# A decoder layer on one core: last products added by VectorE, low halves read later, a first variance by squares, gate products behind Silu alone

## The reference

```python
# 1. attention-like mixing
Xn = layernorm(X) * gamma + beta
Q, K, V = split(Xn @ W_in + b_in, 3)
K, V = rotary(K), rotary(V)                       # the first 256 features turned
A = sum over tokens of (K / |K|) * (V / |V|)      # one number per batch and feature
Y = (0.5 * A + 0.5) * Q @ W_out + b_out + X       # x1 = layernorm(x + Y)
# 2. cross product with a context, both quantised to fp8 by their largest value
out = quantised(x1) @ quantised(ctx) + mask       # x2 = layernorm(x1 + out)
# 3. feed-forward with experts
mlp = silu(x2 @ gate_w) * (x2 @ up_w) @ down_w
routing: product keys, the 8 best of 64 x 64 pairs per token, index into 1024 rows
experts = sum over 8 rows of silu(x2 . down_row) * softmax(score) * up_row
result = layernorm(x2 + mlp + experts)
```

## Time and profile before

| | us |
|---|---|
| median of 3 runs | 812.98 (812.97 to 815.38) |
| profiled execution, its own time | 813.83 |
| span of the profiled execution | 812.0 |
| TensorE busy | 786.8 (97%) |
| VectorE busy | 675.4 (83%) |
| GpSimd busy | 372.2 (46%) |
| ScalarE busy | 314.4 (39%) |

### The profile page before, as it was taken

The page is one execution under the profiler, slowest core; times in us unless marked ns, Lnnn a source line. Parts: engine busy times, 40 slices in busy tenths (PEclk is TensorE's granted clock), DMA queues, the critical chain, the costliest instruction groups (busy, mean ns, idle before and its releaser), DMA issues. The chain is left out here.

```text
span 812.0 us, 10715 instructions
## 1 busy us (share of the span) xinstructions
PE 786.8 (97%) x3631; PEld 644.5 (79%) x3631; DVE 675.4 (83%) x1331; ACT 314.4 (39%) x688; POOL 372.2 (46%) x303
## 2 busy tenths in 40 slices
PE   8999999998899999999999999999999999999995
PEld 6878888887777778888888888888878877878784
DVE  6887679895799782277679999999999999999997
ACT  6444347353564413212343333333333333333322
POOL 1332122232233221113468667776666667677432
PEclk9999999997999999999999999999999999999998
DMA  8567505544446329100023231322333334222113
GB/s 321 223 144 168 104 17 126 144 105 78 54 129 147 63 96 315 44 1 31 30 78 90 83 91 39 120 71 67 99 94 89 92 92 115 70 79 71 37 55 153
DMA packets 51336, 81.70 MB, mean 101 GB/s; under 512 B 17520, under 2 KB 26480, under 8 KB 50769
## 3 DMA queue, kind: packets, MB, share of 16 engines
q0 software_dynamic: 24384, 33.48, 19.6%
q1 hardware_dynamic: 25312, 47.52, 16.9%
q10 hardware_dynamic: 1584, 0.01, 0.1%
HBM read 110.44 MB, written 12.58 MB: 151 GB/s over the span
## 5 line engine op out<-in xcount | busy, mean ns | idle before, releaser
L1718 PE MATMUL gu<-x_hi,w_hi 128*128 128x512 f32 x528 | 206.9, 392 | 2.2 <-DVE mid L1488 1.8
L1720 PE MATMUL gu<-x_hi,w_lo 128*128 128x512 f32 x528 | 205.5, 389 | 0.0
L1719 PE MATMUL gu<-x_lo,w_hi 128*128 128x512 f32 x528 | 205.5, 389 | 0.0
L1237 POOL TENSOR_TENSOR h_lo<-mid,h_hi 128x512 fp32r<-128x512 f32 x62 | 80.2, 1315 | 106.9 <-ACT h_hi L1357 106.4
L1367 ACT ACTIVATE gates<-dots 128x1 f32<-128x1 f32 x144 | 29.3, 203 | 232.2 <-DVE dots L1579 229.3
L1718 PEld LDWEIGHTS gu<-x_hi,w_hi 128*128 128x128 f32 x528 | 99.1, 188 | 25.2 <-DVE mid L1488 4.4
L1720 PEld LDWEIGHTS gu<-x_hi,w_lo 128*128 128x128 f32 x528 | 99.1, 188 | 20.9
L1719 PEld LDWEIGHTS gu<-x_lo,w_hi 128*128 128x128 f32 x528 | 99.2, 188 | 20.1
L1256 POOL DMA_INDIRECT ctx_q<-table_dram,row_i x64 | 80.4, 1256 | 62.2 <-DVE xall L1588 42.5
L1256 POOL DMA_INDIRECT scratch<-table_dram,row_i x64 | 82.8, 1293 | 39.5 <-issue 21.4
L1718 PE MATMUL ob<-w_hi,h_hi 128*128 128x512 f32 x248 | 97.4, 393 | 2.4 <-POOL h_lo L1237 2.4
(11 more groups left out here) (214 smaller groups left out, 1404.4 us busy)
## 6 DMA issues: line engine op xcount, KB each, us to landing
stage<-in_ctx SPq DMA_DIRECT2D x7, 1024.0 KB, 6.2
total<-prod POOLq DMA_DIRECT2D x12, 512.0 KB, 4.7
xall<-half_bo POOLq DMA_DIRECT2D x4, 1024.0 KB, 10.1
xhat<-in_L_ffn_gate_w SPq DMA_DIRECT2D x8, 512.0 KB
xhat<-in_L_ffn_up_w SPq DMA_DIRECT2D x8, 512.0 KB
xall<-in_mask_Bx1xS_ff POOLq DMA_DIRECT2D x4, 1024.0 KB, 10.8
xhat<-in_L_ffn_down_w SPq DMA_DIRECT2D x8, 512.0 KB
x_dram<-xall SPq DMA_DIRECT2D x4, 1024.0 KB, 8.4
```

Source lines behind the costliest of these rows:

```text
L1237: nc.gpsimd.tensor_tensor(lo[:, c], mid[c][:], hi[:, c].bitcast(F32), ALU.subtract).then_inc(hlo_done, 1)
L1718: nc.tensor.matmul(dst, lhs[0], rhs[0], start=start, stop=False)
L1719: nc.tensor.matmul(dst, lhs[0], rhs[1], start=False, stop=False)
L1720: return nc.tensor.matmul(dst, lhs[1], rhs[0], start=False, stop=stop)
```

## The change

- The last tile's products of the last batch no longer go through GpSimd's DMA: VectorE adds `prod` to `total` (`last_total`) when the second DMA has landed, and signals `total_all`, for which `token_sums(LAST)` waits. On VectorE the residuals 2 and 3 and their variance come ahead of this, `ctx_quantise(3)` behind it, and `low_ffn` behind `low_y`. On ScalarE `copy_sums(LAST)` comes behind two centres and scales.
- Products with a low part come later: in `key_value` (batch 0, and tile 0 of the others), in tile 0 of `attention`, in the first gate product of units 0 to 2, and in tile 0 of `down` and `down_early`. TensorE waits for the high part first, and for the low part ahead of its own products.
- The first batch's variance in the second block: the residual also sums its output, a one-column operation makes minus the mean (`minus_first`), ScalarE squares the centred tile and sums it (`deviation`), VectorE makes the variance (`first_variance`). Its transposes go to `ob`, those of the other batches stay in `gu`. Transposes of batch 1 and the cross products of batch 0 alternate. ScalarE's `scaled(1, (2, 3))` comes behind `high_x2(0)`.
- The low parts of the first down and query weights move from GpSimd to VectorE (`first_low_w`); GpSimd's next `low_w` waits for them.
- From unit 5 on the gate products wait for `silu_done` of the unit before, and the up products for `mid_done`.
- `keep_running`: 10 for 6 at the end of the first block; 5, 3 times 7, 4 and 3 for 8, 3 times 10, 4, 8 and 4 at the start of the second.

The core of the diff (16 columns of indentation are taken off; "..." marks what is left out):

```diff
-    add_products(b, 3)
+        add_products(b, 3)
...
 query(LAST, 0)
 query(LAST, 1)
-copy_sums(LAST)
 for i in range(2):
     centre_x1(LAST - 1, i)
     scale_x1(LAST - 1, i)
+copy_sums(LAST)
...
+def last_total():
+    dve.wait_ge(total_in, 16 * (3 * LAST + 2))
+    dve.wait_ge(prod_done, NT)
+    nc.vector.tensor_tensor(total[:], total[:], prod[:, (TB - 1) % 2], ALU.add).then_inc(total_all, 1)
...
-ctx_quantise(3)
 residual(LAST - 1, 2)
 residual(LAST - 1, 3)
 variance(range(TB))
-for s, part in enumerate((gate_s[0], up_s[0])):
-    low_ffn(s, part)
+last_total()
+ctx_quantise(3)
 largest_late(0)
 largest_late(1)
 multiplier(LAST)
 for c in range(KC):
     low_y(LAST, c)
+for s, part in enumerate((gate_s[0], up_s[0])):
+    low_ffn(s, part)
...
+def key_value_high(b, i, k):
...
+    pe.wait_ge(hi_done, KC * part_of_tile(b, i) + k + 1)
+            pe.wait_ge((w_hi_done, w_lo_done)[part], k + 1)
...
+def first_key_value(b):
+    for k in range(KC + 1):
+        if k < KC:
+            key_value_high(b, 0, k)
+        if k:
+            key_value_low(b, 0, k - 1)
...
+    if b == LAST:
+        pe.wait_ge(total_all, 1)
...
+    if i == 0:
+        for k in range(KC):
+            pe.wait_ge(yhi_done, KC * b + k + 1)
+            nc.tensor.matmul(att_bank(b, i)[:], y_hi[:, k, ts], wo_hi[:, k], start=(k == 0), stop=False)
+            nc.tensor.matmul(att_bank(b, i)[:], y_hi[:, k, ts], wo_lo[:, k], start=False, stop=False)
+        for k in range(KC):
             pe.wait_ge(ylo_done, KC * b + k + 1)
-        last = three(att_bank(b, i)[:], y_hi[:, k, i * P:(i + 1) * P], y_lo[:, k, i * P:(i + 1) * P], wo_hi[:, k], wo_lo[:, k], k == 0, k == KC - 1)
...
-keep_running(6)
+keep_running(10)
...
+def x2t_bank(b, i):
+    return (gu if b else ob)[i]
...
-pool.wait_ge(l2_done, TB)
-low_w(2, 0, 2, 0)
-low_w(3, 0, 3, 1)
...
+def deviation(i):
+    act.wait_ge(minus_first, i + 1)
+    if i:
+        act.wait_ge(squared, i)
+    nc.scalar.activation(junk2[:], tile(i), ACT.Square, bias=z_minus[:, i:i + 1], accum_out=z_square[:, i:i + 1]).then_inc(squared, 1)
...
-scaled(1, range(TB))
+scaled(1, (0, 1))
+for i in range(TB):
+    deviation(i)
 for n in range(TB - 1):
     high_x2(n)
     if n == 0:
+        scaled(1, (2, 3))
...
+def first_residual(i):
+    dve.wait_ge(cross_mm, i + 1)
+    dve.wait_ge(xm_in[0], 16)
+    own.did(nc.vector.scalar_tensor_tensor(tile(i), ob[i][:], unscale[:], tile(i), ALU.mult, ALU.add, accum_out=z_sum[:, i:i + 1]))
+    own.wait()
+    nc.vector.tensor_scalar(z_minus[:, i:i + 1], z_sum[:, i:i + 1], -1.0 / D, None, ALU.mult).then_inc(minus_first, 1)
+
+def first_variance(k):
+    cols = slice(2 * k, 2 * k + 2)
+    dve.wait_ge(squared, 2 * k + 2)
+    nc.vector.tensor_scalar(var2[:, cols], z_square[:, cols], 1.0 / D, LN_EPS, ALU.mult, ALU.add).then_inc(v3_ready, 1)
+
+def first_normalise(i):
+    dve.wait_ge(r3_ready, i // 2 + 1)
+    nc.vector.tensor_scalar(tile(i), tile(i), z_minus[:, i:i + 1], rstd2[:, i:i + 1], ALU.add, ALU.mult).then_inc(x2_done, 1)
...
+def first_low_w(m, r, slot):
+    dve.wait_ge(whi_done, m + 1)
+    hi, lo = parts(0, r)
+    nc.vector.tensor_tensor(flat(lo, r), stage_of(r, slot), flat(hi, r).bitcast(F32), ALU.subtract).then_inc(wlo_done, 1)
...
-residual(0, (0, 1))
-variance((0, 1))
-residual(0, (2, 3))
-variance((2, 3))
-normalise(0, (0, 1))
-normalise(0, (2, 3))
+for i in range(TB):
+    first_residual(i)
+first_variance(0)
+first_variance(1)
+for i in range(TB):
+    first_normalise(i)
 low_x2(0)
 quantise(1, range(TB))
 for n in range(TB - 1):
     middle(n, 0)
+    if n == 0:
+        first_low_w(2, 2, 0)
     residual(n + 1, range(TB))
     variance()
...
             quantise(n + 2, (3,))
+            if n == 0:
+                first_low_w(3, 3, 1)
...
+    if n < TB - 1 and c == 0:
+        pe.wait_ge(h2_done, TB * (n + 1))
+        if n:
+            pe.wait_ge(l2_done, TB * n + 1)
+        else:
+            pe.wait_ge(y_done, TB + 2)
+        for k in range(KC):
+            for h in range(2):
+                nc.tensor.matmul(gu[0][:], gate_s[g_set][h][:, k, fs], x2_hi[:, k, cols], start=(k == 0 and h == 0), stop=False)
+        pe.wait_ge(l2_done, TB * (n + 1))
+        for k in range(KC):
+            last = nc.tensor.matmul(gu[0][:], gate_s[g_set][0][:, k, fs], x2_lo[:, k, cols], start=False, stop=(k == KC - 1))
...
+    if up_free is not None:
+        pe.wait_ge(mid_done, up_free)
...
-    pe.wait_ge(hlo_done, GC * n + GC)
+    pe.wait_ge(hhi_done, GC * n + GC)
+    h, (w_high, w_low) = h_of(n), down_s[g_set]
-            last = three(ob[i][:], [h[:, c, ts] for h in h_of(n)], [w[:, c] for w in down_s[g_set]], c == 0, c == GC - 1)
+            nc.tensor.matmul(ob[i][:], h[0][:, c, ts], w_high[:, c], start=(c == 0), stop=False)
+            nc.tensor.matmul(ob[i][:], h[0][:, c, ts], w_low[:, c], start=False, stop=False)
+        if i == 0:
+            pe.wait_ge(hlo_done, GC * n + GC)
+        for c in range(GC):
+            last = nc.tensor.matmul(ob[i][:], h[1][:, c, ts], w_high[:, c], start=False, stop=(c == GC - 1))
...
-keep_running(ob[3], 8)
-cross(0, nothing)
-transposes(1, range(TB), own_bank, x1t_mm, freed(y_done, 0))
+keep_running(ob[3], 5)
+for i in range(TB):
+    transposes(1, (i,), own_bank, x1t_mm, freed(y_done, 0))
+    cross(0, nothing, (i,))
+pe.wait_ge(y_done, TB + 2)
-    pe.wait_ge(z2_done, i + 1)
-    keep_running(ob[0], 10)
+    pe.wait_ge(minus_first, i + 1)
+    keep_running(gu[0], 7)
-keep_running(ob[0], 4)
-transposes(0, range(TB), own_bank, x2t_mm, freed(y_done, TB), x2_done)
-keep_running(ob[0], 8)
-pe.wait_ge(l2_done, 2)
-keep_running(ob[0], 4)
+keep_running(gu[0], 4)
+x2_transposes(0, nothing)
+keep_running(gu[0], 3)
-    pe.wait_ge(l2_done, TB * (n + 1))
...
-            pe.wait_ge(mid_done, GC * (n - 1) + c + 1)
-        gate_up(n, g % 2, tb, c, load_index(g, 1) + 1 if tb == 0 and c == 0 else None)
+            pe.wait_ge(silu_done, GC * (n - 1) + c + 1)
+        gate_up(n, g % 2, tb, c, load_index(g, 1) + 1 if tb == 0 and c == 0 else None, up_free=GC * (n - 1) + c + 1)
```

More of the change, by code:

```diff
@@ L951, in attention @@
                         pe.wait_ge(z_done, TB * (b - 1) + 3 + i)
-                    for k in range(KC):
-                        if i == 0:
+                    ts = slice(i * P, (i + 1) * P)
+                    if i == 0:
[4 more added lines that the diff above has]
+                        for k in range(KC):
                             pe.wait_ge(ylo_done, KC * b + k + 1)
-                        last = three(att_bank(b, i)[:], y_hi[:, k, i * P:(i + 1) * P], y_lo[:, k, i * P:(i + 1) * P], wo_hi[:, k], wo_lo[:, k], k == 0, k == KC - 1)
+                            last = nc.tensor.matmul(att_bank(b, i)[:], y_lo[:, k, ts], wo_hi[:, k], start=False, stop=(k == KC - 1))
+                    else:
+                        for k in range(KC):
+                            last = three(att_bank(b, i)[:], y_hi[:, k, ts], y_lo[:, k, ts], wo_hi[:, k], wo_lo[:, k], k == 0, k == KC - 1)
                     last.then_inc(att_mm, 1)
@@ L968, in _ @@
                             transposes(1, c)
-                    key_value(0, 0, k)
-                    key_value(0, 1, k)
+                    if k == KC - 1:
+                        for i in range(2):
+                            key_value_high(0, i, k)
+                            key_value_low(0, i, k - 1)
+                            key_value_low(0, i, k)
+                        break
+                    for i in range(2):
+                        key_value_high(0, i, k)
+                    for i in range(2):
+                        if k:
+                            key_value_low(0, i, k - 1)
                 pe.wait_ge(s_const, 32)
@@ L974, in _ @@
                     if b:
-                        for i in range(2):
+                        first_key_value(b)
+                        for i in range(1, 2):
                             for k in range(KC):
                                 key_value(b, i, k)
-                                if b > 1 and i == 1 and k >= 2:
+                                if b > 1 and k >= 2:
                                     token_sums(b - 1, range(4 * (k - 2), 4 * (k - 1)))
@@ L1720, in three, with x2_transposes, transposes @@
                     return nc.tensor.matmul(dst, lhs[1], rhs[0], start=False, stop=stop)
-                def transposes(b, tiles, bank, count, free, ready=None):
+                def x2_transposes(b, free):
+                    for i in range(TB):
+                        free(i)
+                        pe.wait_ge(x2_done, TB * b + i + 1)
+                        for c in range(KC):
+                            j = TB * b + i
+                            last = nc.tensor.transpose(x2t_bank(b, i)[:, c * P:(c + 1) * P], xall[:, j * D + c * P:j * D + (c + 1) * P], ident[:])
+                        last.then_inc(x2t_mm, 1)
+                def transposes(b, tiles, bank, count, free):
                     for i in tiles:
```

(18 more changed lines are left out.)

57 lines of the change are left out of this document (34 added, 23 removed).

## The result

| | median of the runs | profiled execution | its span |
|---|---|---|---|
| before | 813.82 us (4 runs) | 813.83 us | 812.0 us |
| changed | 802.54 us (4 runs, 802.24 to 802.84) | 802.24 us | 800.4 us |

The ratio is 0.9877, with a 95% interval of 0.9846 to 0.9908: faster by 1.2%. The forecast was 802.7.

A forecast was written before the change was run, and what follows sets the result against it. TensorE was taken to bound the first half, VectorE's expert work to lead the second. Terms 0.8 + 7.3 + 1.9 + 0.3 = 10.3 us gave 803.5 profiled, 802.7 median, range 799.8 to 807.3.

The forecast's parts named there:

- B: Last batch's token sums: VectorE adds the last products, so TensorE's wait and the clock drop go; gain 7.3 us.
- A: First products: waiting later for low halves saves 0.4 and 0.75, some 0.4 given back; gain 0.8 us (0.2 to 1.2).
- C: Start of the second block: faster residuals and variance, earlier mask, shorter down_early stalls; gain 1.9 us (0 to 3.5).
- it lands 1.0 earlier: Mask's DMA holding residual(1): issued 1.0 us earlier behind the second power, so landing 1.0 earlier.
- 3.5 if it is early enough: Upper bound, in us, of the gain at the second block's start, if the mask lands early enough.
- D: Expert units: gate products wait for Silu alone, down for h_hi; gain 0.3 us (0 to 4.9), since VectorE leads.
- R3: Rival: TensorE's stalls in the expert units are its own and all go, 4.9 instead of 0.3; 798.1 us; 7%.
- R4: Rival: VectorE's dots and GpSimd's low parts block each other 0.6 more in 21 units; slower, 815.3 us; 4%.
- R1: Rival: the clock drops all the same at the last token sums; gain there 5.7, time 807.3 us; 13%.
- R2: Rival: filler too thin at the second block's start, unit 0's 24 products at 1.2 GHz; 805.2 us; 10%.
- R5: Rival: total still waits for its second DMA, the clock drops, other gains at lower bounds; 0.2, 812.8 us; 2%.

The follow-up runs named there:

- experiment 1: The kernel before with only the changed last products: VectorE adds them, ctx_quantise(3), low_ffn and copy_sums moved; 805.95 us, ratio 0.9929.
- 3: The changed kernel with the third accumulating DMA of the last batch and the old order restored; 809.78 us, ratio 0.9972.
- experiment 2: The kernel before with 20 filler transposes between query(LAST, 1) and the last token sums, DMA unchanged; 808.64 us, ratio 0.9960.
- experiment 4: The changed kernel with gate products among the experts waiting for mid again and down for h_lo; median 801.59 us, profiled execution 806.16.
- 8: The changed kernel with GpSimd's low_w of the expert units cut to one column of eight elements; 795.95 us, ratio 0.9803.
- 12: The changed kernel with the expert units' low parts on VectorE and batch 0's token sums one chunk later; 795.80 us, ratio 0.9807.
- 10: The changed kernel with expert low parts on VectorE, and without the looser waits of gate products and down; 795.90 us.
- experiment 5: The changed kernel with the first four tiles' variance by BN_STATS again; 803.91 us, ratio 0.9892.
- experiment 7: The changed kernel without its filler transposes in the second block (5 + 21 + 4 + 3); 804.51 us, ratio 0.9906.
- first series: The timing series of the first four follow-up kernels, beside the kernel before on its chip, whose median was 812.86 us.

## Why the prediction was right, and where it was not

**B, 7.3 for 7.5: right step by step.** Total ready at 184.0 (forecast 185.0), clock held, power up to 3.03, the copy of the sums in time. The 1.2 by which `last_total` might have delayed GpSimd's mean did not show: the mean runs beside it, from 183.03, and takes 1.04 (1.03 before). `residual(LAST, 0)` was late by 0.65 (1.0) and the delay made up at the last one (214.44 to 206.00, 8.44 earlier). Experiments 1 and 3 isolate the step, 2 splits it.

**A, 0.8 for 0.94: close by two misses against each other.** The first products of all gave 0.22 (42.24 to 42.02) for 0.4, and the place at 48.06 gave 0.71 for 0.75. The sum then counted 0.4 given back at the first sums. In the profiled execution nothing was: the DMA, issued at 54.41, had landed by 59.50. It is a matter of tenths: experiment 4's execution waited there 1.0 and paid 4.5. The prediction priced this meeting as a wait and left out the clock behind it.

**C, 1.9 for 3.85: the term "it lands 1.0 earlier" for the mask's DMA was mis-sized.** Measured, behind A and B, the mask's landing came 2.9 earlier, for two reasons. The residuals ended 0.7 earlier (0.88 a tile for 1.05), and with them the issue. And the landing, from issue, took 12.9 us in the profiled execution of the kernel before, 11.7 in the changed one, 11.8 and 12.0 in experiments 1 and 2, which have the old stage C, and 11.3 to 12.0 in the ten others. So 12.9 was that one execution's, not the kernel's, and the bound "3.5 if it is early enough" was the likelier. Who holds `residual(1)` was not the error: `cross` and the mask are level. In the changed kernel's own execution it is `cross`, in experiments 3, 4 and 8 to 12 the mask, for 0.79 to 1.14 us. Against experiment 1's execution C gives 3.4 (`mid` of unit 2, 285.58 to 281.23, less A's 0.94). `down_early` gave 0.47 and 0.44, as forecast. The first gate product came 11.15 earlier (238.50 to 227.35), 11 by the forecast.

**D, 0.3 for about -0.7.** The reading of who leads was right (R3 falls by experiments 4, 8 and 10). That R4 decides "from 0.5 per unit on" was the wrong question: the lock between VectorE and GpSimd moved once, at the first final normalisation, for 0.97. The argument "GpSimd's order hangs on ScalarE and VectorE alone" overlooked that `h_hi` waits for `down_mm`, TensorE's. Another 0.25 went at 422 us, where a blocked dot took 1.16 instead of 0.89; this is not D's, since the dot takes 1.14 in experiment 4 too, and 0.88 in experiment 5, which has D. Its cause stays open.

R1 and R2 did not occur; experiment 7 forces R2 and finds about its price. R5 falls.

The forecast's 802.7 for 802.54 is closer than its terms, and that is luck: C gave 1.95 more than its term and D with what lies behind it 1.0 less, the terms sum to 10.3, and 11.6 was measured against the profiled 813.83, while the medians of before lay at 812.98, later 813.82. On the chip of the first series the executions compared spread from 808.24 to 815.06, and those below 809 have a mean granted clock of 0.995 instead of 0.986 to 0.992. Their time is that of experiment 2, which has the wait without the drop; no trace was taken of one, so that they are executions in which the clock held is likely and not shown.

## What to carry to other kernels

Price a wait of TensorE with the clock behind it: look at the granted clock after each idle stretch, in stages of 1 us, since a slice of the page (20 us here) can hide a drop. If the wait can't go, fill it (20 transposes won 4.2 of 7.5 us here). When another engine leads, look for what blocks that engine, before loosening waits of the one that follows: loosening gave nothing, moving 15 subtractions from GpSimd to VectorE gave 6.6 us. And take a transfer's duration from several executions before calling it what holds a step.

## What the hardware showed unexpectedly

- Behind 1.0 us of idle time (before 60.7, experiment 4) the clock fell once to 0.50, for some 7 us; behind 2.5 us (186, the kernel before) for some 10 us, amid small products. In the changed kernel waits of 0.8 to 1.45 elsewhere passed without a drop, in stages of 1 us too.
- The kernel before has a third drop, to 0.50 from 223 to 226 us, amid waits of 1.3 and 1.1 us, and its clock row shows a 9 there. It delayed nothing on VectorE, and the changed kernel has none there.
- Twenty transposes of 128 columns in a row, 2.35 us, kept 1.00.
- One operation of 128x1024 on VectorE takes 1.23 us with no subtraction of GpSimd beside it (the addition `last_total`), and 2.58 in the mean as a subtraction beside GpSimd's `h_lo`. A normalisation of four tiles, which has one SBUF tensor as input, takes 1.91 alone and 2.88 beside an `h_lo`.
- GpSimd is held too: its power of 128x4 takes 3.03 us beside `ctx_quantise` and 1.96 beside `low_ffn`.
